# Attention's start in a fused Trainium2 kernel: fewer maxima ahead of the loop, mask rows in short packets

## The chip, the cores and the metric

One core of one Trainium2 chip. The metric is device time in microseconds (us), the median of three runs. A core has five engines with a queue each: PE (TensorE, matrix products), DVE (VectorE), ACT (ScalarE), POOL (GpSimd) and SP (SyncE, which here only issues DMAs). ACT and POOL issue DMAs too. Each works through its own instructions in the order in which they were written, and waits on semaphores for the others.

## The reference, cut to what matters

```
x = x + 0.5 * ffn(layernorm(x))     # x: (8, 256, 256), float32
x = x + attn(layernorm(x))
x = x + 0.5 * ffn(layernorm(x))

attn: 16 heads of 16, 4 groups of keys and values (4 heads share one), causal
  q, k, v = xn @ Wq + bq, xn @ Wk + bk, xn @ Wv + bv
  p = softmax(where(key > query, -inf, q k^T / 4));  out = p v
ffn: 8 experts, the best one for each row
  (silu(x @ gate[e]) * (x @ up[e])) @ down[e] * sigmoid(router score)
```

## The kernel before

The program has three stages: a first layer of experts, attention, a second layer of experts. Each expert layer (`ffn_pe`, `ffn_act`, `ffn_dve`, `ffn_pool`) gathers the rows of an expert in tiles of 128, multiplies them by weights that stay in SBUF, and scatters the result; it is PE's stage. The change leaves its products alone and touches its two borders with attention.

Attention goes through 8 batches b of 256 rows, with 4 groups of heads each, so 32 groups m, n = 0 to 31. For one batch, before any group of it:

- layernorm gives `xn`, `ln_transpose` (PE, L534) turns it, `ln_evacuate` (ACT, L542) copies it out of PSUM;
- `a_proj_q` (L1261) and `a_proj_kv` (L1269) are the projections, in float32; ACT adds the bias to the queries (`a_split_act`, L1296), DVE to the keys (`a_split_k`, L1327); the values' half goes by ACT (`a_vt_act`, L1279) and back to PE (`a_vt_pe`, L1286), and DVE adds their bias (`a_split_v`, L1332);
- queries and keys are split into three bfloat16 parts each (`a_split_act2`, L1307 and L1309; `a_split_dve2`; `a_split_act3`; `a_split_dve3`, L1348), and SP and ACT lay the parts one above the other with DMAs, "stacks" (`a_stack_q`, L1358, `a_stack_k`, L1366): 96 rows of `Qs` and `Ks`, in a ring of three batches.

For one group of heads, first the row maxima: `a_max_pe(m, k)` for k = 0, 1, 2 is one chunk of scores into one of two banks (two L1421 and an L1423 for the causal mask, or four L1414 and an L1418), `a_max_dve(m, k)` reduces it (L1451 or L1447). When a batch's maxima are there they are negated and turned (`a_neg_dve`, `a_neg_pe` L1468, `a_neg_copy` L1480), and SP puts them into row 103 of `Qs` (`a_max_row`, L1397). Rows 96 to 102 of `Qs` and 96 to 103 of `Ks` are constant "mask rows", `qrows` and `krows`, which SP loads once from HBM (L1624, L1625). Then the scores proper over all 104 rows, less maxima and mask: `a_scores(n, u)`, u = 0, 1, 2 (L1499), the exponentials (`a_exp`, ACT, L1506, the first with a table load), the causal cut on POOL (`a_mask`), the product with the values (`a_values`, L1527 and L1530), ACT's copy, PE's transposes (`a_heads_pe`, L1556), and DVE's division and addition into `xt` (`a_heads_sum`, `_div`, `_add`, L1576).

The order is written out by hand, for each engine apart. Ahead of the loop come the maxima of seven groups, m = 0 to 6, with the preparation of batches 1 and 2 between them. Then the loop: step n has the scores of group n + 1, the values of n, and the maxima of m = n + 7. A batch's stack must have landed before its first maxima (`a_max_pe` waits on `a_qs`).

SP's queue at attention's start: batch 0 of the first layer's result (`load_middle(0)`, L1611), as soon as the scatters of all but the last tile have landed; after the last scatter (`s_fin`) batches 1 to 4; stack 0; batches 5 to 7; the two mask rows; stack 1; then maxima rows and stack 2.

The scores of a group wait for the mask rows by one line:

```
                    if (m, k) == (NG + 1, 2):
                        pe.wait_ge(s_one, 32)
                        pe.wait_ge(a_v, 2)
                        for u in range(3):
                            a_scores(0, u)
```

Of the kernel before, what the change touches and what calls it, by code (L numbers as in the profile page):

```python
# [33 lines left out]
BA = 5  # L34
# [21 lines left out]
MAX_ORDER = (1, 0, 2)  # L56

EARLY = 3
WARM_MID = 5
WARM_NEXT = 26  # L60
WARM_FRONT = 7
# [78 lines left out]
def block_rows():  # L140
# [4 lines left out]
    return q, k  # L145


def macaron(nc, x, wq, bq, wkv, bk, bv, router, wall, constf, constb, qrows, krows,
            out):
    with ExitStack() as ctx:  # L150
# [147 lines left out]
        s_one = sem("s_one")  # L298
        dve = sem("dve")
# [497 lines left out]
        def warm(n, ps=bank[3]):  # L797

            for i in range(n):
                nc.tensor.matmul(ps[:], identb, cstb("mask"), start=True, stop=True)  # L800
# [171 lines left out]
        def ffn_gate_up(l, j, off):  # L972
# [6 lines left out]
            for m, done in ((0, f_gp), (1, f_up)):  # L979
# [12 lines left out]
                last.then_inc(done[l], 1)  # L992

# [67 lines left out]
        def ffn_pe(l):  # L1061
# [41 lines left out]
        def ffn_act(l):  # L1103
# [34 lines left out]
            for j in range(NP):  # L1138
                if j == 0:
# [3 lines left out]
                    else:  # L1143
                        ln_evacuate(2, B - 1, bank[4])
# [23 lines left out]
        def first_norm(seen):  # L1168


            for t in range(*tiles(1, 0)):
                ln_sums(1, t, seen)
# [4 lines left out]
        def ffn_dve(l, seen):  # L1177
# [40 lines left out]
            for j in range(NP):  # L1218
                if l == 1 and j == 0:
                    normalise(l, 0)  # L1220
# [81 lines left out]
        def a_split_act2(b):  # L1302
# [4 lines left out]
            a.copy(qp[:, b % 2, 0], q32[:]).then_inc(a_qh, 1)  # L1307
            a.wait_ge(a_k32, b + 1)
            a.copy(kp[:, b % 2, 0], k32[:]).then_inc(a_qh, 1)  # L1309

# [129 lines left out]
        def a_max_dve(m, k):  # L1440
# [8 lines left out]
            else:  # L1449
                h0 = HG * g + 2 * (u - 1)  # L1450
                v.tensor_reduce(mxa[:, b % 2, 1, h0:h0 + 2],  # L1451
                                o[:].rearrange("p (h k) -> p h k", h=2), AX.X, ALU.max).then_inc(a_am, 1)

# [131 lines left out]
        def _(sp):  # L1585
# [27 lines left out]

            load_middle(0)
            sp.wait_ge(s_fin[0], 1)
# [14 lines left out]
            a_stack_k(sp, 1, 2)  # L1630
            a_max_row(sp, 0)
# [10 lines left out]
        def _(p):  # L1642
# [10 lines left out]
            ln_apply(3, p)  # L1653
            a_split_dve2(2, p)
            a_split_dve3(2, p)
            a_mask(0)
            for n in range(NG * B):
                if n + 1 < NG * B:
                    a_mask(n + 1)
                b, g = divmod(n, NG)  # L1660
# [15 lines left out]
        def _(a):  # L1676
# [22 lines left out]
            a_split_act2(1)  # L1699
# [6 lines left out]
            a_vt_act(2, PRO_KV[2])  # L1706
            a_split_act2(2)
            a_split_act3(2)
# [311 lines left out]
```

## Time and profile before

| | |
|---|---|
| median of 3 runs | 404.71 us (404.37 to 405.14) |
| the profiled execution | 407.15 us |
| its span, first to last instruction | 405.4 us |
| mean granted TensorE clock | 0.977 of full |
| PE busy | 367.1 us (91%) |
| DVE busy | 241.9 us (60%) |
| ACT busy | 144.0 us (36%) |
| POOL busy | 172.7 us (43%) |

The profile is one execution; all its times count from the start of its span. A busy share is an average over stages: the first expert layer runs to about 126 us, attention from there to about 294 us, the second layer to the end. Matmuls are pipelined, so a row's duration is longer than the distance to the next row's start; the distance is what an instruction costs PE. A value in square brackets behind a row is how long the engine sat idle before it, and what ended that.

### The profile page before, as it was taken

The page shows a single profiled execution, that of the slowest core. Times are in us where ns is not written, and L with a number is a line of the kernel's source. Part 1 is how long each engine was busy: PE and PEld are TensorE (multiplying, and loading weights), DVE is VectorE, ACT ScalarE, POOL GpSimd, SP SyncE. Part 2 cuts the span into 40 slices and gives each one's busy share as a digit, 9 for nine tenths or more (in the row PEclk, how much of TensorE's full clock was granted, in tenths as well). Part 3 has the DMA queues.
Part 4 walks back from the last instruction along what each step waited for, and adds up shares of the span by engine and source line. Part 5 has one row for each costly group of instructions (what it writes and reads, how often), then busy time and mean ns, then how long its engine had stood idle before and what let it go on. Part 6 is the DMA issues. An engine that isn't in the chain of part 4 may idle for free.

```text
span 405.4 us, 8372 instructions
## 1 busy us (share of the span) xinstructions
PE 367.1 (91%) x3128; PEld 291.2 (72%) x3134; DVE 241.9 (60%) x725; ACT 144.0 (36%) x296; POOL 172.7 (43%) x284
## 2 busy tenths in 40 slices
PE   8999999999994868989999999998799999999980
PEld 6769999999962445646666565654499999999660
DVE  5889943222214656877878778889847875222220
ACT  3222111111111332776676657677334111111110
POOL 1040425544121252665867664565822214653111
PEclk9999999999999997999999999999989999999995
DMA  8969841279301761312314042200121102398100
GB/s 263 408 205 384 295 154 59 74 262 320 145 25 47 197 155 49 100 42 57 83 45 125 11 116 71 59 28 28 52 66 34 46 21 60 90 361 321 44 24 15
DMA packets 27055, 50.04 MB, mean 123 GB/s; under 512 B 4458, under 2 KB 20590, under 8 KB 25975
## 3 DMA queue, kind: packets, MB, share of 16 engines
q1 hardware_dynamic: 19118, 25.10, 19.4%
q0 software_dynamic: 4512, 21.50, 15.5%
q10 hardware_dynamic: 3376, 2.80, 2.3%
q8 instruction: 29, 0.48, 0.5%
q14 instruction: 20, 0.16, 0.1%
HBM read 35.16 MB, written 6.55 MB: 103 GB/s over the span
## 4 chain that ended last, share of the span: by engine, by line
PE 69%; DVE 16%; DMA 5%; issue 4%; SPq 2%; ACT 1%; POOL 1%; ACTq 1%; POOLq 0%; DVEq 0%
PE bank L990 26%; PE bank L1035 13%; PE bank L1527 3%; PE bank L1499 3%; PE bank L1261 3%; PE bank L1421 3%; DVE mxa L1451 2%; PE bank L534 2%; PE bank L1007 2%; PE bank L957 2%; PE bank L1414 2%; PE bank L1556 2%; PE bank L584 1%; DVE area L1576 1%; PE bank L1530 1%
## 5 line engine op out<-in xcount | busy, mean ns | idle before, releaser
L990 PEld LDWEIGHTS bank<-area,W 128*128 128x128 f32 x1024 | 120.6, 194 | 2.5 <-ACT area L1111 1.1
L990 PE MATMUL bank<-area,W 128*128 128x128 f32 x1024 | 121.5, 277 | 0.2 <-ACT area L1111 0.2
L1201 DVE TENSOR_TENSOR area<-area,bank 128x512 f32<-128x512 f32 x34 | 23.4, 688 | 68.2 <-issue 52.7
L1506 ACT ACTIVATE area<-bank 128x512 f32<-128x512 f32 x96 | 54.1, 597 | 23.1 <-PE bank L1499 22.6
L1035 PE MATMUL bank<-W,area 128*128 128x256 f32 x256 | 61.0, 381 | 0.4 <-DVE area L1186 0.4
L1515 POOL TENSOR_SCALAR_AFFINE_SELECT area<-area 128x512 f32<-128x512 f32 x64 | 40.9, 653 | 39.0 <-ACT area L1506 38.7
L1122 ACT ACTIVATE area<-bank 128x512 f32<-128x512 f32 x34 | 20.3, 597 | 101.8 <-PE bank L990 93.2
L1035 PEld LDWEIGHTS bank<-W,area 128*128 128x128 f32 x256 | 46.1, 190 | 6.8 <-issue 1.8
L1451 DVE TENSOR_REDUCE mxa<-bank 128x2 f32<-128x512 f32 x64 | 42.9, 672 | 9.3 <-PE bank L1423 9.1
L884 POOL DMA_INDIRECT x2d<-area,sidx x17 | 17.1, 1008 | 55.7 <-DVE area L1186 55.7
L884 POOL DMA_INDIRECT out<-area,sidx x17 | 17.1, 1007 | 52.9 <-DVE area L1186 52.1
L1186 DVE SCALAR_TENSOR_TENSOR area<-bank,ms,area 128x256 f32<-128x256 f32 x34 | 16.4, 481 | 30.8 <-PE bank L1035 26.2
L1499 PE MATMUL bank<-area 104*128 104x512 bf16 x96 | 34.7, 380 | 0.0
L1111 ACT COPY area<-bank 128x256 f32<-128x256 f32 x34 | 12.7, 372 | 55.0 <-PE bank L957 55.0
L872 POOL DMA_INDIRECT area<-x,gidx x18 | 18.5, 1029 | 29.9 <-DVE sidx L691 20.0
L1447 DVE TENSOR_REDUCE mxa<-bank 128x4 f32<-128x512 f32 x32 | 22.0, 688 | 12.7 <-PE bank L1434 12.0
L1421 PE MATMUL bank<-area 96*128 96x256 bf16 x128 | 25.7, 284 | 0.7 <-DVE mxa L1451 0.3
L872 POOL DMA_INDIRECT area<-rows,gidx x18 | 17.5, 974 | 14.2 <-PE bank L990 7.6
L1527 PE MATMUL bank<-area,V 128*32 128x256 f32 x256 | 20.5, 390 | 0.6 <-issue 0.6
L534 PE MATMUL bank<-cf,area 128*128 128x128 f32 x96 | 15.4, 284 | 4.8 <-DVE area L519 2.6
L542 ACT COPY area<-bank 128x512 f32<-128x512 f32 x16 | 9.4, 586 | 26.4 <-PE bank L534 26.3
L1421 PEld LDWEIGHTS bank<-area 96*128 96x128 bf16 x128 | 9.0, 100 | 13.4 <-DVE mxa L1447 5.1
(198 smaller groups left out, 568.3 us busy)
## 6 DMA issues: line engine op xcount, KB each, us to landing
W<-wall SPq DMA_DIRECT2D x24, 512.0 KB, 6.9
area<-area SPq DMA_DIRECT2D x48, 128.0 KB, 2.4
area<-x SPq DMA_DIRECT2D x8, 256.0 KB, 5.3
area<-x2d SPq DMA_DIRECT2D x8, 256.0 KB, 3.0
rows<-area ACTq DMA_DIRECT2D x8, 256.0 KB, 2.4
area<-JV SPq DMA_DIRECT2D x40, 32.0 KB, 1.9
cb<-constb ACTq DMA_DIRECT2D x1, 296.0 KB, 4.4
area<-x,gidx POOLq DMA_INDIRECT x18, 3.4
```

Source lines behind the costliest of these rows:

```text
L534: last = nc.tensor.transpose(o[:, c, i * P:(i + 1) * P], src[:, i, c * P:(c + 1) * P], ident)
L872: nc.gpsimd.indirect_dma_start(dst, None, table, bass.IndirectOffsetOnAxis(ap=gidx[:, bass.ds(j, 1)], axis=0)).then_inc(done, 16)
L884: nc.gpsimd.indirect_dma_start(ffn_out[l], bass.IndirectOffsetOnAxis(ap=sidx[:, bass.ds(t, 1)], axis=0), ob[:, j % OB, :], None, bounds_ch ...
L990: last = pe.matmul(ps[:, i * P:(i + 1) * P], W[:, w:w + P], xT[:, j % 2, c, :], start=(c == 0), stop=(c == C - 1))
L1035: last = pe.matmul(ps[:, 0:H], hT[:, n % 2, i, :], W[:, bass.ds(off + at, H)] if mixed(l, n) else W[:, off + at:off + at + H], start=(i == ...
L1201: v.tensor_tensor(out, sil[:, n % 2, :], bank[2 + n % 2][:], ALU.mult).then_inc(f_h[l], 1)
L1421: pe.matmul(o[:, h * S:(h + 1) * S], Qs[0:KROWS, r, HG * g + 2 * (u - 1) + h, P:S], Ks[0:KROWS, r, g, :], start=(h == 0), stop=False)
L1451: v.tensor_reduce(mxa[:, b % 2, 1, h0:h0 + 2], o[:].rearrange("p (h k) -> p h k", h=2), AX.X, ALU.max).then_inc(a_am, 1)
L1499: pe.matmul(o, Ks[0:MROWS + 1, r, g, k0:k0 + P], rhs, start=True, stop=True).then_inc(a_st, 1)
L1506: a.activation(PT[:, n % 2, u * 512:(u + 1) * 512], bank[u][:], ACT.Exp, scale=D ** -0.5).then_inc(a_e, 1)
L1515: p.affine_select(out=src, in_=src, compare_op=ALU.is_ge, fill=0.0, base=0, pattern=[[0, HG], [1, P]], channel_multiplier=-1).then_inc(a_p ...
L1527: pe.matmul(bank[5][32 * h:32 * h + 32, c0:c0 + S], V[:, b % VB, 0, g, :], PT[:, n % 2, h * S:(h + 1) * S], start=True, stop=False, tile_p ...
```

## The change

It has seven parts, all at attention's borders:

1. PE and DVE do the maxima of four groups (m = 0 to 3) ahead of the scores of group 0, not seven. The three first steps are written out (`early_step_pe`, `early_step_dve`), with two groups of maxima each; from n = 3 on the loop is the old one.
2. The scores of group 0 wait for three mask-row DMAs (`s_one` of 48). They are cut into packets of 2 KB (`ROWX`); `krows` and the first batch's `qrows` are issued behind `load_middle(0)`, the rows of the other two batches behind stack 1 and the loads of batches 5 to 7, which are themselves behind stack 1 now.
3. PE does the first two chunks of maxima ahead of batch 1's transposes.
4. ACT adds the bias of batches 1 and 2's keys (`a_split_k_act`), not DVE.
5. ACT does the exponentials of group 0 ahead of splitting batch 2; POOL its first mask ahead of that batch's `a_split_dve2`.
6. At the end of the first layer DVE's `ln_sums` of batch 0 come ahead of the last `finish`.
7. At the start of the second layer DVE's `normalise(1, 0)` comes ahead of the last group's heads, PE's last `ln_transpose` between the gate and the up products of tile 0, and ACT's last `write_rows` behind `copy_tile(0)`.

```diff
@@ block_rows
-    return q, k
+    return (x.reshape(len(x), -1, ROWX).transpose(1, 0, 2) for x in (q, k))
@@ ffn_gate_up
                 last.then_inc(done[l], 1)
+                if l == 1 and j == 0 and m == 0:
+                    ln_transpose(2, B - 1, bank[4])
@@ ffn_pe
                         warm(2, bank[2])
-                    else:
-                        ln_transpose(2, B - 1, bank[4])
@@ ffn_act
                     else:
+                        write_rows(a, B - 1)
                         ln_evacuate(2, B - 1, bank[4])
@@ ffn_dve
+            if l == 0:
+                for t in range(*tiles(1, 0)):
+                    ln_sums(1, t, seen)
             finish(NP - 1)
@@ new, scalar
+        def a_split_k_act(b, ps):
+            a = nc.scalar
+            a.wait_ge(a_kv, b + 1)
+            a.wait_ge(a_qr, 2 * b)
+            a.activation(k32[:], ps[0:NG * D, 0:S], ACT.Identity, bias=bk_s[:]).then_inc(a_k32, 1)
@@ new, tensor
+        def early_step_pe(n):
+            pe = nc.tensor
+            groups = early_groups(n)
+            a_scores(n + 1, 0)
+            if n == 0:
+                pe.wait_ge(a_ms, 2)
+                ln_transpose(1, 3, PRO_T[3])
+            a_max_pe(*groups[0])
+            if n == 0:
+                a_vt_pe(2, PRO_KV[2])
+            if n == 2:
+                pe.wait_ge(a_v, 4)
+                a_neg_pe(2)
+            a_scores(n + 1, 1)
+            if n == 1:
+                a_vt_pe(3)
+            a_max_pe(*groups[1])
+            a_scores(n + 1, 2)
+            a_max_pe(*groups[2])
...
@@ sync
+            def load_qrows(r0, r1):
+                n = NH * S // ROWX
+                sp.dma_start(Qs[KROWS:MROWS, r0:r1].rearrange("o r h s -> o (r h s)").rearrange(
+                    "o (c x) -> o c x", x=ROWX), qrows[n * r0:n * r1].rearrange("c o x -> o c x")).then_inc(s_one, 16)
             load_middle(0)
+            sp.wait_ge(s_used, 1)
+            sp.dma_start(Ks[KROWS:MROWS + 1].rearrange("o r g s -> o (r g s)").rearrange("o (c x) -> o c x", x=ROWX),
+                         krows.rearrange("c o x -> o c x")).then_inc(s_one, 16)
+            load_qrows(0, 1)
             sp.wait_ge(s_fin[0], 1)
...
-            for b in range(BA, B):
-                load_middle(b)
-            sp.dma_start(Ks[KROWS:MROWS + 1].rearrange("o r g s -> o (r g s)"), krows).then_inc(s_one, 16)
-            sp.dma_start(Qs[KROWS:MROWS].rearrange("o r h s -> o (r h s)"), qrows).then_inc(s_one, 16)
             a_stack_q(sp, 1, 0)
             a_stack_k(sp, 1, 0, slice(2, 3))
             a_stack_q(sp, 1, 1)
             a_stack_q(sp, 1, 2)
             a_stack_k(sp, 1, 2)
+            for b in range(BA, B):
+                load_middle(b)
+            load_qrows(1, QB)
             a_max_row(sp, 0)
@@ scalar
             a_split_act(2, PRO_Q[2])
-            a_vt_act(2, PRO_KV[2])
-            a_split_act2(2)
-            a_split_act3(2)
-            ln_evacuate(1, 3, PRO_T[3])
             for u in range(3):
                 a_exp(0, u)
+            a_split_act2(2, PRO_KV[2])
+            a_vt_act(2, PRO_KV[2])
@@ tensor
             warm(WARM_NEXT)
-            ln_transpose(1, 1, PRO_T[1])
             a_vt_pe(0, PRO_KV[0])
             for m in range(NG):
                 for k in range(3):
                     a_max_pe(m, k)
                     if (m, k) == (0, 1):
+                        ln_transpose(1, 1, PRO_T[1])
                         a_proj_q(1, PRO_Q[1])
...
+            pe.wait_ge(s_one, 48)
+            pe.wait_ge(a_v, 2)
+            for u in range(3):
+                a_scores(0, u)
+            a_neg_pe(1)
+            for n in range(RAMP):
+                early_step_pe(n)
+            for n in range(RAMP, NG * B):
```

How the order changes, at three places. Line numbers in the changed kernel differ (L1266 and L1274 are the projections, L1291 `a_vt_pe`, L537 the layernorm's transposes, L1427 to L1436 the maxima, L1581 the scores, L1550 `a_neg_pe`). First PE's queue behind the fill products of attention's start, before:

```order
L800 MATMUL bank<-cb 128x512 x26
L534 MATMUL bank<-cf,area 128x128 x4
L1286 MATMUL bank<-cf,vT 128x64 x2
L1421 MATMUL bank<-area 128x256 x2
L1423 MATMUL bank<-cb 128x2x128
L1414 MATMUL bank<-area 128x128 x4
L1418 MATMUL bank<-cb 128x512
L1261 MATMUL bank<-area,wq_s 128x256 x4
```

and in the changed kernel:

```order
L803 MATMUL bank<-cb 128x512 x26
L1291 MATMUL bank<-cf,vT 128x64 x2
L1434 MATMUL bank<-area 128x256 x2
L1436 MATMUL bank<-cb 128x2x128
L1427 MATMUL bank<-area 128x128 x4
L1431 MATMUL bank<-cb 128x512
L537 MATMUL bank<-cf,area 128x128 x4
L1266 MATMUL bank<-area,wq_s 128x256 x4
```

The four transposes of batch 1 went from ahead of the first two chunks of maxima to behind them, right ahead of the projection that reads them.

Second, SP's queue, from the first loads to the first row of maxima, before:

```order
L1611 DMA area<-x2d 128x2x256 x5
L1358 DMA area<-area 16x8x512 x3
L1366 DMA area<-JV 16x4x256 x2
L1358 DMA area<-area 16x8x512 x3
L1611 DMA area<-x2d 128x2x256 x3
L1624 DMA area<-krows 8x3072
L1625 DMA area<-qrows 7x12288
L1358 DMA area<-area 16x8x512 x3
L1366 DMA area<-JV 16x4x256
L1358 DMA area<-area 16x8x512 x3
L1366 DMA area<-JV 16x4x256
L1397 DMA area<-mT 1x8x256
```

and in the changed kernel:

```order
L1693 DMA area<-x2d 128x2x256
L1703 DMA area<-krows 8x3x1024
L1698 DMA area<-qrows 7x4x1024
L1693 DMA area<-x2d 128x2x256 x4
L1371 DMA area<-area 16x8x512 x3
L1379 DMA area<-JV 16x4x256 x2
L1371 DMA area<-area 16x8x512 x6
L1379 DMA area<-JV 16x4x256
L1371 DMA area<-area 16x8x512 x3
L1379 DMA area<-JV 16x4x256
L1693 DMA area<-x2d 128x2x256 x3
L1698 DMA area<-qrows 7x8x1024
```

One third of the query mask rows went ahead of stack 0; three loads and the other two thirds went behind stack 1. The row of maxima (L1410 there) comes next.

Third, ACT's queue from batch 2's queries on, before:

```order
L1296 ACTIVATE area<-bank,bq_s 128x256 x2
L1279 COPY vT<-bank 64x256
L1307 CAST area<-area 128x512
L1309 CAST JV<-k 64x256
L1314 CAST area<-area 128x512
L1316 CAST JV<-kr 64x256
L542 COPY area<-bank 128x512
L1506 ACT_TABLE_LOAD
L1506 ACTIVATE area<-bank 128x512 x6
```

and in the changed kernel:

```order
L1301 ACTIVATE area<-bank,bq_s 128x256 x2
L1588 ACT_TABLE_LOAD
L1588 ACTIVATE area<-bank 128x512 x3
L1312 CAST area<-area 128x512
L1322 ACTIVATE k<-bank,bk_s 64x256
L1316 CAST JV<-k 64x256
L1284 COPY vT<-bank 64x256
L1588 ACTIVATE area<-bank 128x512
L545 COPY area<-bank 128x512
```

Batch 2's values (the COPY to `vT`) and its first split stand behind three exponentials now, with the keys' bias (L1322) between them.

## Rows read from the trace of the kernel before

**Rows 1.** Stretches: start:end, length, busy us of each engine, PEclk (granted clock), DMA share, GB/s

```profile
142.00:147.00 5.00, 4.94 (x36) 4.04 (x35) 3.53 (x14) 2.04 (x4) 1.61 (x9) 1.00 0.78 204
147.00:151.00 4.00, 0.45 (x4) 0.20 (x2) 2.11 (x4) 1.02 (x3) 3.56 (x6) 1.00 0.51 84
152.00:158.00 6.00, 5.52 (x23) 3.44 (x21) 3.90 (x9) 0.59 (x1) 1.84 (x2) 0.50 0.31 83
161.50:181.50 20.00, 17.92 (x165) 10.71 (x165) 15.81 (x37) 14.46 (x30) 12.82 (x16) 1.00 0.24 63
199.00:216.70 17.70, 16.69 (x175) 11.12 (x174) 14.39 (x41) 11.87 (x27) 12.42 (x25) 1.00 0.29 82
```

**Rows 2.** Timeline of PE, 141 to 186 us: start, duration, instruction

```profile
141.74 0.66 PE L534 MATMUL bank<-cf,area 128*128 128x128 f32 x4 [1.58 <-DVE area L519]
142.59 0.39 PE L1421 MATMUL bank<-area 96*128 96x256 bf16 x2
...
143.38 1.89 PE L1261 MATMUL bank<-area,wq_s 128*128 128x256 f32 x8
...
150.78 0.34 PE L1286 MATMUL bank<-cf,vT 64*128 64x64 f32 x2 [3.55 <-ACT vT L1279]
...
160.85 0.27 PE L1423 MATMUL bank<-cb 128*128 128x256 bf16 x1
...
165.30 0.81 PE L1499 MATMUL bank<-area 104*128 104x512 bf16 x3
...
185.86 0.42 PE L1527 MATMUL bank<-area,V 128*32 128x256 f32 x4
```

**Rows 3.** Timeline of ACT at attention's start; ACTq is its DMA issues

```profile
142.43 0.59 ACT L542 COPY area<-bank 128x512 f32<-128x512 f32 x1 [2.90 <-PE bank L534]
...
147.01 0.40 ACT L1309 CAST JV<-k 64x256 bf16<-64x256 f32 x1 [0.22 <-DVE k L1327]
147.44 2.82 ACTq L1366 DMA_DIRECT2D area<-JV  x2
...
151.71 1.20 ACTq L1366 DMA_DIRECT2D area<-JV  x2
...
166.44 3.33 ACT L1506 ACTIVATE area<-bank 128x512 f32<-128x512 f32 x6
```

**Rows 4.** Timeline of SP's DMA issues

```profile
122.81 0.38 SPq L1611 DMA_DIRECT2D area<-x2d  x1
...
140.77 1.67 SPq L1611 DMA_DIRECT2D area<-x2d  x3
142.94 0.29 SPq L1625 DMA_DIRECT2D area<-qrows  x1
```

**Rows 5.** DMA packets of 142.5:144 (first two) and 144:146 us (last two)

```profile
DMA packets 517, 0.50 MB, mean 333 GB/s; under 512 B 29, under 2 KB 517, under 8 KB 517
q1 hardware_dynamic: 517, 0.50, 100.6%
...
DMA packets 276, 0.46 MB, mean 230 GB/s; under 512 B 27, under 2 KB 261, under 8 KB 269
q1 hardware_dynamic: 276, 0.46, 111.3%
```

**Rows 6.** DMA issues of 122 to 125.5 us: KB each, median us from issue to landing

```profile
area<-x2d SPq DMA_DIRECT2D x1, 256.0 KB, 2.7
```

**Rows 7.** Timeline of DVE: last tile, first row of maxima, two reductions

```profile
125.93 0.48 DVE L1186 SCALAR_TENSOR_TENSOR area<-bank,ms,area 128x256 f32<-128x256 f32 x1 [3.39 <-PE bank L1031]
126.33 0.74 DVE L381 BATCH_NORM_STATS2 bn<-area 128x6 f32<-128x256 f32 x2
...
153.25 0.27 DVE L1480 COPY mT<-bank 8x256 bf16<-8x256 bf16 x1
...
167.76 1.29 DVE L1451 TENSOR_REDUCE mxa<-bank 128x2 f32<-128x512 f32 x2
```

**Rows 8.** Timeline of DVE at the second layer's start

```profile
293.14 0.41 DVE L1165 TENSOR_SCALAR area<-area,ms 128x256 f32<-128x256 f32 x1
```

More of the change, by code:

```diff
@@ L56 @@
 MAX_ORDER = (1, 0, 2)
+ROWX = 1024
 EARLY = 3
@@ L60 @@
 WARM_NEXT = 26
+RAMP = 3
 WARM_FRONT = 7
@@ L799, in warm @@
             for i in range(n):
-                nc.tensor.matmul(ps[:], identb, cstb("mask"), start=True, stop=True)
+                last = nc.tensor.matmul(ps[:], identb, cstb("mask"), start=True, stop=True)
+            return last
         def idle(n):
@@ L1168, in first_norm @@
         def first_norm(seen):
-            for t in range(*tiles(1, 0)):
-                ln_sums(1, t, seen)
             ln_stats(1, 0, seen)
@@ L1452, in a_max_dve, with early_groups, early_step_dve @@
                                 o[:].rearrange("p (h k) -> p h k", h=2), AX.X, ALU.max).then_inc(a_am, 1)
+        def early_groups(n):
+            return [(NG + 2 * n + i, k) for i in range(2) for k in range(3)]
+        def early_step_dve(n, seen):
+            for i, (m, k) in enumerate(early_groups(n)):
+                a_max_dve(m, k)
+                if (n, i) == (0, 0):
+                    a_split_v(2, PRO_KV[2])
+                if (n, i) == (1, 0):
+                    a_split_k(3)
+                if (n, i) == (1, 1):
+                    a_split_v(3)
+                if (n, i) == (2, 0):
+                    a_neg_copy(2)
+                    a_heads_sum(0, seen)
+                if (n, i) == (2, 1):
+                    a_heads_div(0, seen)
+                if (n, i) == (2, 2):
+                    a_heads_add(0, seen)
+            if n == 1:
+                a_neg_dve(2)
+                a_split_dve2(3)
+            if n == 2:
+                round_stats_next(0, seen)
+                round_aggr(0, seen)
+                round_eps(0, seen)
+                round_guess(0, seen)
+        def early_step_pe(n):
[8 more added lines that the diff above has]
+                a_vt_pe(2, PRO_KV[2])
+            if n == 2:
+                pe.wait_ge(a_v, 4)
+                a_neg_pe(2)
+            a_scores(n + 1, 1)
+            if n == 1:
+                a_vt_pe(3)
+            a_max_pe(*groups[1])
+            a_scores(n + 1, 2)
+            a_max_pe(*groups[2])
+            if n == 0:
+                pe.wait_ge(a_q32, 3)
+                a_proj_q(3, bank[7], (0,))
+                a_max_pe(*groups[3])
+                pe.wait_ge(a_v, 3)
+                a_values(0)
+                a_proj_q(3, bank[7], (1,))
+                a_max_pe(*groups[4])
+                a_proj_kv(3)
+            else:
+                a_values(n)
+                a_max_pe(*groups[3])
+                a_max_pe(*groups[4])
+            a_max_pe(*groups[5])
+            if n >= 1:
+                pe.wait_ge(a_q32, 4)
+                a_heads_pe(n - 1)
         def a_neg_dve(e):
@@ L1737, in _ @@
                     ln_evacuate(1, b + 4, bank[6])
-            write_rows(a, B - 1)
             ffn_act(1)
@@ L1797, in _ @@
             a_neg_dve(1)
-            a_split_k(2, PRO_KV[2])
-            for m in range(NG, NG + 3):
-                for k in range(3):
-                    a_max_dve(m, k)
-                    if (m, k) == (NG, 0):
-                        a_neg_copy(1)
-                    if (m, k) == (NG, 2):
-                        a_split_v(2, PRO_KV[2])
-            for n in range(NG * B):
+            a_neg_copy(1)
+            for n in range(RAMP):
+                early_step_dve(n, seen)
+            for n in range(RAMP, NG * B):
                 b, g = divmod(n, NG)
@@ L1857, in _ @@
                 a_heads_add(n, seen)
+                if n == NG * B - 2:
+                    normalise(1, 0)
             ffn_dve(1, seen)
@@ L1995 @@
     cf, cbf = constants()
+    qrows, krows = block_rows()
     import ml_dtypes
```

41 lines of the change are left out of this document (16 added, 25 removed).

## The prediction, made before the changed kernel ran

> **What bounds the kernel now.** I read the stretches first, then each engine's timeline where a stretch is thin. In the loop PE is busy 16.69 of 17.70 us for one batch at full clock and DVE 14.39 [rows 1]: PE's work sets that pace, and the loop from n = 3 on isn't changed, so what the change gains or loses must arise ahead of step 3 or at the two borders, and the loop hands it on in full. The thin stretch is 147 to 151 us, with 0.45 us of PE work; from 152 to 158 the granted clock is 0.50, so PE runs at 1.2 GHz, the lower of its two levels, behind that gap [rows 1]. PE's timeline shows the gap as one wait of 3.55 us for ACT's copy of the values [rows 2]. ACT had issued two DMAs ahead of it, which took 2.82 us; a later pair took 1.20 [rows 3]. The query mask rows went out at 142.94, shortly before [rows 4].
>
> How heavy those rows are follows from the packets. In 142.5 to 144, 517 packets fill 16 engines: 24 engine-us, 0.047 each. In 144 to 146, 276 packets fill 111.3% of 32, 35.6 engine-us; 269 of them at 0.047 make 12.6, so the 7 of over 8 KB take 23, about 3.3 us each [rows 5]. They run until about 148.5, and the stacks of batch 1 (issued from 146.8) meet them. I take the 1.6 us (2.82 less 1.20) for their doing.
>
> **The change, part by part,** as shifts against the old times.
>
> *DVE's sums ahead of the last `finish`.* `load_middle(0)` goes out at 122.81 and takes 2.7 [rows 4, 6]: the data is there at 125.5. Two sums take 0.74; `finish` starts at 126.25, not 125.93 [rows 7]. The last scatter, and the loads and stack 0 behind it, come **0.3 later**.
>
> *Chunks ahead of batch 1's transposes.* The first chunks can't start before stack 0, so at 142.6 + 0.3 = 142.9. Two chunks take 0.79 (142.59 to 143.38), so the transposes start at 143.7. ACT's copy now starts 0.7 behind the transposes' start (141.74, 142.43) and takes 0.59 [rows 2, 3]: the projection starts at 143.7 + 1.35 = 145.05, **1.7 later**. Before, that copy lay beside the chunks.
>
> *Keys by ACT.* ACT's cast of the keys (147.01) was waiting 0.22 for DVE [rows 3]. Its own 0.48 in line adds **0.3**. So the cast is at 149.0, and with 0.43 to the issue and 1.20 for the pair without the stall the values' copy starts at 150.6, PE's `a_vt_pe` at 151.05, against 150.78. The stall's 1.6 are eaten by the 2.0: **0.3 later**.
>
> *The clock.* PE's gap there is now about 2 us (a projection that starts 1.7 later ends later too), so I take full clock for what follows. From 150.78 to the last chunk of m = 3 (160.85, over at 161.1) are 10.3 us [rows 2]. The 5.52 us of busy time at 0.50 would be half, 2.8 [rows 1]; a little of that comes back as waits for DVE. I take **2.6 earlier**. PE is through with m = 3 at 161.1 + 0.3 - 2.6 = 158.8.
>
> *The mask rows behind stack 1.* The scores of group 0 now follow at once and wait for all three mask DMAs. The last is issued so: the first row of maxima at 153.25 [rows 7] as before (0.3 later, 0.25 earlier by the clock), 1.1 for DVE's V and third part of the queries, 1.2 for two stack issues, then 1.67 for three loads [rows 4]: 157.2. Its landing isn't in the trace. Below, it isn't faster than a load, 2.7 [rows 6]; above, the old one, about 5.6 (142.94 to 148.5). It carries two thirds of the bytes to the same 7 partitions, 2/3 of 3.3 = 2.2, behind loads that end some 2.1 behind its issue: 4.3. I take that, nearer the old row, since it is the same transfer cut smaller: it lands at 161.5, and PE **waits 2.7**. The first row of maxima is issued behind it and does not come sooner.
>
> The Trainium skill (DMA: Bandwidth & Descriptors, "Why a DMA increments its semaphore by 16 and not by 1") says that a DMA is spread by the outermost dimension of its two sides, and that is 7 partitions here, in 2 KB packets too; then the landing is the 4.3. Were the packets spread over all 16 engines, the landing would be a load's 2.7 and the sum 1.6 lower.
>
> *The ramp.* Before, from the first scores (165.30) to the values of group 4 (185.86) are 20.56 us [rows 2], with 17 chunks of maxima between them (the rest of m = 6, m = 7 to 10, two of m = 11). Now there are 23 (m = 4 to 10, two of 11). Six more cost 6 x 0.395 = 2.4; the transposes of batch 3, `a_vt_pe(2)` and `a_neg_pe(1)`, which stood ahead of the scores, bring 0.44, 0.27 and 0.22 of PE work: 3.3. To this come waits that the old order didn't have. `a_vt_pe(2)`, in the first early step, waits for ACT, which has three exponentials (3.33 / 6 = 0.55 each), a cast of the queries (an estimate: the same 128x512, 0.55), the keys (0.48) and the 0.4 cast ahead of the copy [rows 3]: with 0.4 for the scores, 3.5 us after their start, when PE has had 1.9 of work: 1.6. `a_vt_pe(3)` waits for DVE's keys behind a chunk, about 1. And an early step holds six reductions of 0.65 (two in 1.29) [rows 7] and three small operations, some 4.3 us of DVE, beside some 3.9 of PE: 0.4 in each of two steps. Sum: 20.56 + 3.3 + 2.6 + 0.8 = 27.3, so the values of group 4 start at 161.5 + 27.3 = 188.8, against 185.86: **2.9 later**. Bounds of the ramp: 21.8 (without waits: PE idles 2.1 of 20 us in the old stretch [rows 1], so 20.56 + 3.3 - 2.1) to 29.
>
> *The second layer's start.* `normalise(1, 0)` at 293.14 [rows 8] stood behind the last heads, 0.6 of DVE; ahead of them it brings the first product up to 0.6 forward. But the last transposes, 0.44, then lie between products instead of beside ACT's copy. **0.1 earlier**; bounds 0 and 0.6. `write_rows` moves on ACT behind a copy and is wanted two tiles later, nothing.
>
> *The clock again.* PE now sits idle 2.7 us for the mask rows and has waits on both sides. A gap of 3.55 brought the lower level [rows 1, 2]; a gap of this size may. It would cost between 0 and the 2.6 above; I take **0.6**, little, since ACT and DVE pace part of that stretch.
>
> Sum: 2.9 - 0.1 + 0.6 = **+3.4 us**. Against the profiled execution's 407.15 that is 410.55; it lies 2.44 above the median of 404.71, so for the median 408.1.
>
> **The rivals.**
>
> *A. The ramp runs at PE's pace (faster).* If the mask rows have landed by 158.8 and the extra chunks fill the waits for exponentials, the ramp is its lower bound and half of the old waits, 22.8: the values of group 4 start at 181.6, 4.3 earlier, and with the border's 0.1 that is 400.3. For it speaks that the old stretch mostly lacks ready work, not PE time. Against it: ACT's queue puts batch 2 behind group 0. It decides where the last mask rows land within 1.6 us of their issue, sooner than any load here. Chance 0.12.
>
> *B. The mask rows come in time, the ramp's waits remain.* A landing of 2.7 or less leaves 1.1 of the wait: +1.8; with no clock loss, +1.2: 405.9. Chance 0.2.
>
> *C. The stall isn't the packets' doing (the change doesn't do what it says), or it comes back behind the new mask rows.* The pair on ACT takes 2.82 again, PE's gap is 3.6, and the clock falls once more: 1.6 and up to 2.6 on top, less what the wait for the mask rows hides (2.7, all but 1.5): +4.9: 409.6, and up to 411. Against: the seven long packets are gone. Chance 0.18.
>
> The forecast keeps 0.5.
>
> **How the numbers follow.** The predicted time is the forecast's, 408.1. Its own range, from the landing (2.7 to 5.6) and the clock (0 to 2.6), is 405.9 to 411. B and C lie almost inside; A doesn't. The range of 8 in 10 is 405.0 to 411.0. A measurement of this kernel tells 0.2%, 0.8 us, from no change. Faster by that: A, 0.12. Within it: the low end of B, 0.08. Slower: 0.80.
>
> **What would show it.** Right: PE's wait for the mask rows ahead of the first scores, 2 to 3 us, at 158 to 159; the pair of DMAs on ACT near 1.2; batch 1's first projection near 145; `a_vt_pe(2)` waiting for ACT; the values of group 4 near 188.8; after that the same 17.7 us a batch. Wrong: scores of group 0 that start before 159.5 without a wait, or values of group 4 before 186. If the first is seen and the time is still longer, the ramp's waits alone were the price (B).

## The result, and the profile after

The changed kernel takes 414.54 us (median of 4 runs, 411.98 to 417.0), against 404.92 for the kernel before (404.37 to 406.98, 4 runs): ratio 1.020, 95% interval 1.015 to 1.025, **9.6 us slower**. (The ratio is the comparison's own estimate, with its interval; the quotient of the two medians is 1.024, inside the interval.) The forecast was 3.4 slower, 408.1, with 405.0 to 411.0: right in sign, outside the range.

The profiled execution of the changed kernel took 413.78 us (span 411.9), 0.8 below its median; that of before, 407.15 (span 405.4), lay 2.2 above its own median. So the two traces differ by 6.5 us only; the other 3.0 of the 9.6 are the distances of the two profiled executions from their medians, and no trace shows what makes them.

Stretches of the changed kernel, with the columns of [rows 1]:

```profile
126.00:132.00 6.00, 3.75 (x22) 1.45 (x12) 3.77 (x18) 0.53 (x1) 0.98 (x1) 0.75 0.08 22
...
147.00:151.00 4.00, 1.80 (x15) 1.23 (x13) 2.91 (x5) 2.49 (x7) 3.43 (x7) 1.00 0.29 78
...
152.70:156.50 3.80, 3.65 (x17) 2.65 (x18) 3.17 (x7) 0.58 (x1) 0.98 (x1) 0.55 0.49 131
...
160.00:163.40 3.40, 0.00 (x0) 0.01 (x1) 0.77 (x2) 0.41 (x1) 0.00 (x0) 0.96 0.13 21
163.40:174.00 10.60, 10.53 (x49) 5.55 (x50) 3.24 (x6) 6.41 (x14) 7.18 (x9) 0.53 0.28 75
...
212.60:230.30 17.70, 16.70 (x177) 11.12 (x174) 14.36 (x40) 11.86 (x27) 12.40 (x25) 1.00 0.29 80
```

The loop is what it was: 16.70 us of PE in 17.70. New is that PE stands still for 3.4 us at 160 and then does nearly all of the next 10.6 us of the ramp at 1.2 GHz (their mean granted clock is 0.53). From 152.7 to 156.5 the mean is 0.55. PE's timeline of the same kernel:

```profile
142.73 0.39 PE L1434 MATMUL bank<-area 96*128 96x256 bf16 x2 [1.76 <-DMA area<-area]
...
144.79 1.99 PE L1266 MATMUL bank<-area,wq_s 128*128 128x256 f32 x8 [0.68 <-ACT area L545]
...
150.96 0.34 PE L1291 MATMUL bank<-cf,vT 64*128 64x64 f32 x2 [2.20 <-ACT vT L1284]
...
159.59 0.27 PE L1436 MATMUL bank<-cb 128*128 128x256 bf16 x1
163.42 1.44 PE L1581 MATMUL bank<-area 104*128 104x512 bf16 x3 [3.55 <-DMA area<-mT]
...
194.10 0.64 PE L1609 MATMUL bank<-area,V 128*32 128x256 f32 x8
```

Against [rows 2]: the projection of batch 1 starts at 144.79 (143.38), `a_vt_pe(1)` at 150.96 (150.78), the first scores at 163.42 (165.30), the values of group 4 at 194.10 (185.86). ACT's pair of DMAs takes 1.29 us instead of the 2.82 of [rows 3]:

```profile
149.15 1.29 ACTq L1379 DMA_DIRECT2D area<-JV  x2
```

SP's queue has the loads, the last mask rows and the row of maxima in this order, behind stack 1:

```profile
155.50 1.62 SPq L1693 DMA_DIRECT2D area<-x2d  x3
157.16 0.37 SPq L1698 DMA_DIRECT2D area<-qrows  x1
157.58 0.76 SPq L1410 DMA_DIRECT2D area<-mT  x1
```

**The ledger of the two traces**, in changes of length from landmark to landmark (PE's timeline): first layer up to the last down product +0.6 (123.93 to 124.56, where nothing is changed); from there to the first chunk of maxima -0.5; to `a_vt_pe(1)` 0.0; to the first scores -2.1 (12.46 for 14.52); **to the values of group 4 +10.1** (30.68 for 20.56); the loop -0.3; from the last values to the second layer's first down product -1.4; the rest 0.0. Sum +6.5. The -1.4 is the clock, not the order: in before the first 32 gate and up products ran at 1.2 GHz for most of their length, here none did. First before, then the changed kernel:

```profile
294.00:298.00 4.00, 3.98 (x22) 3.74 (x20) 3.59 (x20) 2.24 (x3) 0.60 (x1) 0.57 0.47 135
```

```profile
302.00:306.00 4.00, 4.00 (x35) 4.00 (x36) 3.59 (x20) 1.45 (x2) 1.52 (x2) 1.00 0.43 133
```

### The profile page after: what moved, and what is told of

Its sections match the earlier page's. It is cut to its first block, busy times and chain, and to the rows that moved or that the text cites. A ratio compares the mean times of both kernels' runs of the same rounds, so it can differ in the third digit from the quotient of the medians.

```text
span 411.9 us, 8362 instructions
## 1 busy us (share of the span) xinstructions
PE 371.8 (90%) x3125; PEld 292.5 (71%) x3125; DVE 240.7 (58%) x723; ACT 144.2 (35%) x298; POOL 171.6 (42%) x284
## 4 chain that ended last, share of the span: by engine, by line
PE 65%; DVE 15%; DMA 7%; issue 4%; ACT 4%; SPq 2%; POOL 1%; ACTq 0%; POOLq 0%; DVEq 0%
PE bank L994 25%; PE bank L1041 13%; DVE mxa L1464 3%; PE bank L1581 3%; PE bank L1266 3%; PE bank L1434 3%; PE bank L1609 3%; PE bank L961 2%; PE bank L537 2%; DMA x2d<-area,sidx 2%; PE bank L1638 1%; DMA area<-mT 1%; PE bank L1427 1%; DMA area<-x2d 1%; PE bank L575 1%
## 5 line engine op out<-in xcount | busy, mean ns | idle before, releaser
L994 PEld LDWEIGHTS bank<-area,W 128*128 128x128 f32 x1024 | 119.0, 192 | 3.0 <-ACT area L1115 1.5
L994 PE MATMUL bank<-area,W 128*128 128x128 f32 x1024 | 120.1, 275 | 0.7 <-ACT area L1115 0.6
L1581 PE MATMUL bank<-area 104*128 104x512 bf16 x96 | 36.1, 395 | 3.5 <-DMA area<-mT 3.5
L537 PE MATMUL bank<-cf,area 128*128 128x128 f32 x96 | 16.7, 302 | 1.9 <-DVE mT L1562 1.6
```

Of the source, the lines that this page charges most:

```text
L537: last = nc.tensor.transpose(o[:, c, i * P:(i + 1) * P], src[:, i, c * P:(c + 1) * P], ident)
L994: last = pe.matmul(ps[:, i * P:(i + 1) * P], W[:, w:w + P], xT[:, j % 2, c, :], start=(c == 0), stop=(c == C - 1))
L1581: pe.matmul(o, Ks[0:MROWS + 1, r, g, k0:k0 + P], rhs, start=True, stop=True).then_inc(a_st, 1)
```

## The experiments

All times come as ratios to the kernel before on the same chip in the same set, since its median moved between sets (406.3 to 410.8 us). The ratios are the comparison's estimates; the quotient of two medians differs from them by up to 0.4% (before_fill: 402.68 by 406.49, 0.991), so a difference of that size between two kernels is no more than a hint. "Ramp" is from the first scores to the values of group 4, "head" from the first chunk of maxima to those values, both from the kernel's profiled execution. Last column: where its trace shows the granted clock at half, 140 to 180 us. A "fill product" (`warm`) is a matrix product of 128x512 whose result nobody reads; it only keeps PE busy, 0.22 us each at full clock. "Theory A" to "E" are those of the expectations.

| kernel | ratio (95%) | ramp | head | half clock from (us) |
|---|---|---|---|---|
| before | 1 | 20.56 | 43.27 | 151.2 |
| changed | 1.020 (1.015 to 1.025) | 30.68 | 51.37 | 152.9, 163.1 |
| rows_first | 1.017 (1.013 to 1.020) | 31.05 | 49.86 | 147.0, 157.2, 167.4 |
| fill_scores | 1.029 (1.024 to 1.034) | 27.68 | 49.79 | 147.2, 157.4 |
| rows_fill | 1.019 (1.015 to 1.023) | 27.69 | 48.43 | 143.8, 157.4 |
| before_rows | 1.009 (1.005 to 1.012) | 20.70 | 43.17 | 152.4, 162.6 |
| new_ramp | 1.013 (1.003 to 1.023) | 27.47 | 45.38 | 152.7 |
| old_ramp | 1.003 (0.998 to 1.007) | 20.57 | 46.45 | 144.7, 155.0, 165.2 |
| borders | 1.002 (0.998 to 1.006) | 20.48 | 42.30 | 144.1, 154.4 |
| before_fill | **0.994** (0.990 to 0.998) | 20.49 | 39.49 | none |
| after_fill | 1.008 (1.004 to 1.013) | 27.67 | 47.66 | 143.2 |
| rows_fill_before | 1.003 (1.000 to 1.007) | 20.55 | 43.33 | 164.5 |
| new_ramp_fill | 1.002 (0.998 to 1.005) | 27.48 | 41.81 | none |
| more_fill | 0.993 (0.990 to 0.997) | 20.49 | 39.49 | none |
| max_row_first | 1.000 (0.996 to 1.004) | 20.49 | 42.96 | 154.1 |
| max_row_fill | **0.993** (0.989 to 0.996) | 20.50 | 39.49 | none |
| no_part3 | 1.004 (1.000 to 1.008) | 27.84 | 43.73 | 152.8 |
| no_part3_fill | 1.000 (0.997 to 1.004) | 27.68 | 43.51 | none |
| next_fill | 1.013 (1.009 to 1.017) | 27.97 | 46.36 | 151.7 |
| row_fill_next | 0.995 (0.992 to 0.998) | 20.49 | 39.49 | none |

A profiled execution is one of the runs, and not always a typical one: that of rows_first lies 4.0 us above its kernel's median, of old_ramp 3.0, of before 2.2 (against 404.92), of after_fill 1.9, and that of row_fill_next 2.7 below; the others lie within 1.4.

### The wait ahead of the first scores

rows_first, on the changed kernel:

```diff
-            for b in range(BA, B):
-                load_middle(b)
             load_qrows(1, QB)
             a_max_row(sp, 0)
+            for b in range(BA, B):
+                load_middle(b)
```

> The changed kernel with the last mask rows and the first row of maxima issued ahead of the loads of batches 5 to 7 (same DMAs, other order on SP). The changed kernel ran at 414.5, with a wait of 3.55 us ahead of the first scores and 10.2 us at a granted clock of 0.5 right behind it. Theory A (the wait for the rows opens the gap, and the gap costs the clock): the wait all but goes (rows issued at about 155.5 instead of 157.2, nothing ahead of them), 3.5 us, and with it most of the low clock, 3 to 4: 407 to 408. Theory B (only the wait, the clock falls anyway): 411. Theory C (the early steps are paced by ACT's and DVE's queues, so that a sooner start is given back in them): 413 or more, first scores at 160 but the values of group 4 no sooner than 192.

fill_scores, and rows_fill (the edit above and `warm(4, ...)`):

```diff
+            warm(16, bank[0])
             pe.wait_ge(s_one, 48)
             pe.wait_ge(a_v, 2)
             for u in range(3):
```

> The changed kernel with 16 fill products (128x512, 0.22 us each at full clock, 3.5 us) on a free bank ahead of the wait for the mask rows; nothing else is moved. PE is then busy where it was idle for 3.55 us. Theory A (the idle gap lowers the clock for the ramp): first scores still at 163.4, but the ramp runs at full clock: 414.5 less 3 to 4.5, 410 to 411.5. Theories B and C (the low clock isn't that gap's doing, or isn't what paces the ramp): 414 to 415.

> Both: rows first and 4 fill products (0.9 us) ahead of the first scores. Theory A: what is left of the wait is filled: 407 to 408, and less spread between runs than the 412 to 417 of the changed kernel. Theory B: 411 to 412. Theory C: 413 to 414.

Measured 1.017, 1.029, 1.019: none came near theory A's 407 to 411. The wait is gone in all three, and in fill_scores and rows_fill the ramp ran at full clock in 27.7 us, 3.0 less than the changed kernel's: that gap did bring the low clock of the ramp. The times are nearest to theory C's (413 or more), but its mechanism, a ramp held by ACT's and DVE's queues, is not what the traces show. All three have the low clock earlier instead, at 144 to 147 and at 157. fill_scores, although its ramp is as short, is the slowest kernel of all. The fill isn't too long for the wait: from `a_vt_pe(1)` to the first scores it takes 12.29 us, 12.46 in the changed kernel. What is longer is the way from the first chunk to `a_vt_pe(1)`, 9.82 against 8.23, with half clock from 147.2; and in its trace the first chunk was already 2.6 later, behind projections at half clock. That is one execution; whether the timed runs lost their time in the same places is not shown. The wait ahead of the scores was only a part of the cost.

### One part at a time, on the kernel before

before_rows is part 2 alone; new_ramp parts 1 and 5 alone; old_ramp all but these two; borders parts 6 and 7. Their edits are pieces of the change's diff. before_fill is new:

```diff
                     if (m, k) == (1, 1):
+                        warm(9, bank[0])
                         a_vt_pe(1, PRO_KV[1])
```

> The kernel before with part 2 of the change alone: mask rows in packets of 2 KB, the first third and krows early, loads of batches 5 to 7 and the rest behind stack 1. Its first scores come later than in the changed kernel (165.3), so the rows are in time. If the long packets made the stall: ACT's pair of DMAs takes 1.2 instead of 2.82, PE's gap shrinks from 3.55 to about 2, 1.6 us sooner, and up to 2.6 more from the clock: 401 to 403.5 against 404.9. If the stall is something else: the pair takes 2.8 again and the time is 404.5 to 405.5.

> The kernel before with parts 1 and 5 of the change alone: four groups of maxima ahead, three written-out steps, ACT's exponentials and POOL's mask of group 0 ahead of splitting batch 2. Mask rows, transposes, keys and both borders as before. At full clock the new ramp took 27.7 us from the first scores to the values of group 4 in two kernels, against 20.56 before, and the first scores come about 4.5 sooner (9 chunks of 0.395 and 0.9 of other work). Theory D (the ramp is the price): ratio to before 1.007 to 1.013 (2.6 for the order, and up to 2.6 for a clock that falls more often in it). Theory E (the new ramp is harmless, the rest of the change does it): 0.998 to 1.002.

> The changed kernel without parts 1 and 5: the old ramp, and parts 2, 3, 4, 6 and 7 of the change. Part 2 alone measured a ratio of 1.009 to before. Theory D: what is left beside the ramp is part 2's and part 3's: 1.008 to 1.013. Theory E: 1.02, as the changed kernel.

> The kernel before with parts 6 and 7 alone (sums ahead of the last finish; second layer's start). By the prediction +0.3 and -0.1, ratio 1.000 (0.999 to 1.001). If the second layer's start is worth more than I took (from the last values to the first down product the changed kernel needed 12.99 us against 14.42 before, of which the lower clock there is 1.7): no more than 0.998. If the sums ahead of the last finish bring the lower clock at 129 us (it was there in all five profiles of kernels with after's start, and not in that of before): 1.003 to 1.006.

> The kernel before with 9 fill products (0.22 us each, 1.9) on a free bank in PE's gap ahead of a_vt_pe(1) (3.55 us), nothing else. If that gap is what lowers the clock behind it in before too: no stretch at 0.50 between 151 and 158, and a ratio of 0.994 to 0.998. If the lower clock comes from the whole of the thin stretch or elsewhere as well: 0.998 to 1.002, and stretches at 0.50 at other places.

The ramp alone costs 1.3%, with a wide interval (four runs): theory D. The borders cost nothing that can be told (1.002, interval over 1); the low clock at 129 isn't part 6's doing, since before_fill, without part 6, has it too, from 129.3. Part 2 alone costs 0.9%, though ACT's stall is gone (pair 1.22 us, `a_vt_pe(1)` 6.59 us behind the first chunk instead of 8.19): neither expectation had that.

old_ramp missed both theories, and the miss matters. It holds parts 2, 3, 4, 6 and 7, and its trace has part 2's stall (DVE waits 1.46 us for the row of maxima, see below) and part 3's half clock at 144.7. Theory D had 1.008 to 1.013; it measured 1.003, and its interval ends at 1.007. So the prices of parts below, taken with the new ramp or alone, don't add up in the old one. Why not stays open.

One group of fill products makes the kernel before faster: at 148 to 151 PE is now busy, and what follows runs at 2.4 GHz, where [rows 1] has a granted clock of 0.50:

```profile
148.00:151.00 3.00, 3.00 (x20) 1.47 (x19) 2.49 (x5) 1.42 (x4) 2.40 (x7) 1.00 0.43 93
151.00:158.00 7.00, 5.85 (x40) 4.25 (x40) 5.40 (x11) 1.89 (x5) 4.11 (x4) 1.00 0.40 108
```

### The same parts with the clock held

The fill ahead of `a_vt_pe(1)` added to the changed kernel (with rows first), to part 2, and to the ramp; and two more fills for before (`WARM_NEXT` 31, and `warm(6, bank[0])` ahead of the second layer).

> The changed kernel with the last mask rows and the row of maxima ahead of the loads of batches 5 to 7, and 8 fill products ahead of a_vt_pe(1), where it waits 2.2 us. The fill alone took before from 406.5 to 402.7 (ratio 0.994). If what the changed kernel pays beyond the ramp's order is the clock: ratio 0.998 to 1.005 (0.994 plus the ramp's 2.1 to 2.9 us). If it pays something else as well: 1.010 or more.

> Part 2 alone on the kernel before, with the same 8 fill products. Part 2 alone measured 1.009, although its stall on ACT was gone and PE reached a_vt_pe(1) 1.6 sooner. If that was paid by the clock alone, the fill takes it back: 0.990 to 0.995. If part 2 itself costs: 0.998 or more.

> Parts 1 and 5 alone on the kernel before, with 9 fill products ahead of a_vt_pe(1): the new order of the ramp with the clock held there. Against the same fill in the old order (0.994), the order's own price is 2.1 to 2.9 us if my sum of it was right: 0.999 to 1.001. If the ramp costs by its lower clock only: 0.994 to 0.996. From first scores to the values of group 4: 27.3 to 27.7 us at full clock.

> The kernel before with 9 fill products ahead of a_vt_pe(1), 31 instead of 26 ahead of batch 1's transposes (PE waits 1.2 to 1.6 us there) and 6 ahead of the second layer (PE waits 1.6). If every thin stretch draws the lower clock: below the 0.994 of the one fill, 0.988 to 0.993, none at 0.50 around 294. If the further fills only delay what stands behind them: 0.995 to 0.998.

**The ramp's order.** With the clock at 1.00 in both, new_ramp_fill's head is 41.81 us against before_fill's 39.49: its ramp is 27.48 against 20.49, and its first scores come 4.67 sooner. That is 2.3 us; the timed ratios, 1.002 against 0.994, say 0.8%, 3.3 us, with intervals of 0.34% and 0.39% to either side. PE's timeline of new_ramp_fill shows where a ramp at full clock waits: for ACT's values of batch 2 (0.74), DVE's keys of batch 3 (1.09), and DVE's reductions ahead of group 4 (1.39):

```profile
157.13 0.81 PE L1577 MATMUL bank<-area 104*128 104x512 bf16 x3
...
160.66 0.33 PE L1287 MATMUL bank<-cf,vT 64*128 64x64 f32 x2 [0.74 <-ACT vT L1280]
...
168.84 0.31 PE L1287 MATMUL bank<-cf,vT 64*128 64x64 f32 x2 [1.09 <-DVE k L1336]
...
182.01 0.39 PE L1430 MATMUL bank<-area 96*128 96x256 bf16 x2 [1.39 <-DVE mxa L1460]
...
184.61 0.64 PE L1605 MATMUL bank<-area,V 128*32 128x256 f32 x8
```

**Part 2.** With the fill it still costs 0.9% (1.003 against 0.994). The trace of rows_fill_before says how, in DVE's timeline and in PE's:

```profile
163.93 0.28 DVE L1483 COPY mT<-bank 16x256 bf16<-16x256 bf16 x1 [2.48 <-DMA area<-mT]
```

```profile
164.86 0.61 PE L1424 MATMUL bank<-area 96*128 96x256 bf16 x2 [2.81 <-DVE mxa L1450]
165.26 0.42 PE L1426 MATMUL bank<-cb 128*128 128x256 bf16 x1
165.47 1.06 PE L536 MATMUL bank<-cf,area 128*128 128x128 f32 x4
```

The first row of maxima was issued at 158.28, behind three loads and the mask rows (before_fill: 155.15). DVE's next copy into the same `mT` waits for it, DVE's reductions queue behind that copy, PE's chunks behind those, and the clock is at half when PE goes on (0.61 for a pair that takes 0.39 at full clock).

**more_fill** is no better than one fill, and the six products ahead of the second layer do harm there: last values to first down product 14.09 us, 12.81 in before_fill.

### The row of maxima, and part 3

max_row_first and max_row_fill are before_rows and rows_fill_before with this edit:

```diff
+            a_max_row(sp, 0)
+            load_qrows(1, QB)
             for b in range(BA, B):
                 load_middle(b)
-            load_qrows(1, QB)
-            a_max_row(sp, 0)
```

> Part 2 alone as in before_rows (1.009), but with the first row of maxima issued directly behind stack 1, ahead of the last mask rows and of the loads of batches 5 to 7. In the profile of part 2 with fill, DVE's copy of the next row of maxima waited 2.48 us for that DMA and PE's maxima waited 2.81 for DVE. If that is part 2's cost: the waits go, and the ratio is 0.997 to 1.002. If part 2 costs by something else (the early mask rows, packets of 2 KB): 1.006 to 1.010 again.

> The same with 8 fill products ahead of a_vt_pe(1). If the row of maxima was part 2's cost: 0.990 to 0.995, no worse than the fill alone (0.994), against 1.003 with the row behind the loads. Otherwise 1.000 to 1.004.

1.000 and 0.993, against 1.009 and 1.003: the place of the row of maxima in SP's queue was part 2's cost, as far as these ratios tell. (The edit takes the last mask rows ahead of the loads as well, but in none of the four traces does PE wait ahead of the first scores, so it isn't they that were late.) In max_row_fill the row is issued at 155.09, DVE's copy does not wait, and the head is the 39.49 of before_fill:

```profile
155.09 0.76 SPq L1400 DMA_DIRECT2D area<-mT  x1
155.89 0.46 SPq L1619 DMA_DIRECT2D area<-qrows  x1
156.39 1.39 SPq L1614 DMA_DIRECT2D area<-x2d  x3
```

max_row_first shows something else. Its mask rows go in packets of 2 KB, and still ACT's pair of DMAs stalls, as it did in before, and PE waits for it:

```profile
150.74 2.48 ACTq L1369 DMA_DIRECT2D area<-JV  x2
...
153.73 0.34 PE L1289 MATMUL bank<-cf,vT 64*128 64x64 f32 x2 [3.21 <-ACT vT L1282]
```

Neither mask rows nor loads were in flight ahead of it: between 146 and 150.7 the trace has a single DMA packet.

no_part3 is rows_first with batch 1's transposes back ahead of the first chunks, no_part3_fill has the 8 fill products too, next_fill is rows_first with `WARM_NEXT` 34, row_fill_next is max_row_fill with `WARM_NEXT` 31.

> The changed kernel with rows first (1.0167), and with part 3 undone: batch 1's transposes are again ahead of the first chunks. By its order part 3 costs 1.7 us; if it also brings the lower clock at 143 to 150, 1 to 2 more: 1.008 to 1.012, no stretch at 0.50 between 140 and 150. If only the 1.7: 1.012 to 1.013. If part 3 costs nothing: 1.016 to 1.018.

> The changed kernel with rows first, part 3 undone and 8 fill products ahead of a_vt_pe(1): the ramp's new order is then all that is left beside the fill. The same ramp on the kernel before measured 1.002 with the fill: 1.000 to 1.004 if parts 4, 6 and 7 are worth nothing either way; against 1.008 with part 3. At 1.007 or more part 3 isn't to blame.

> The changed kernel with rows first (1.0167) and 34 instead of 26 fill products ahead of the first chunks, where PE waits 1.6 to 2.2 us for stack 0 (8 x 0.22 = 1.7). If part 3's cost beyond its order's 1.7 us is the clock that this wait brings down: 1.006 to 1.011 and no stretch at 0.50 between 140 and 150. If the clock falls there for other reasons, or the rest of part 3's cost is no clock: 1.015 to 1.018.

> The kernel before with part 2, the first row of maxima ahead of the loads, 8 fill products ahead of a_vt_pe(1) (0.993), and 31 instead of 26 ahead of batch 1's transposes. If every thin stretch counts: 0.988 to 0.992. If the first fill had all that there is: 0.992 to 0.995.

**Part 3** costs 1.3% with the new ramp (rows_first 1.017, no_part3 1.004), with the fill 0.8% (1.008, 1.000): 3.3 to 5 us. That is more than expected: for no_part3 the lowest expectation was 1.008. after_fill's 1.008 lies between its two theories. In the old ramp it can't be so much (old_ramp, above). The stretch 143.2 to 150 of after_fill and of no_part3_fill, which differ by part 3 alone:

```profile
143.20:150.00 6.80, 5.71 (x20) 4.28 (x21) 2.04 (x10) 0.58 (x1) 2.78 (x13) 0.50 0.01 2
```

```profile
143.20:150.00 6.80, 6.37 (x39) 4.42 (x39) 5.25 (x16) 2.71 (x7) 3.26 (x13) 1.00 0.13 34
```

At half clock PE got through 20 instructions instead of 39. Ahead of it PE had waited 2.27 us for stack 0, and waited another 0.67 for ACT's copy in it; in no_part3_fill the four transposes sit in that wait. Of the seven kernels with part 3 five show half clock that begins between 143 and 147; the two that don't are the changed kernel's profiled execution and next_fill, which fills the wait. Of the thirteen without part 3 one does. next_fill bears this out in part: its clock is at 1.00 from 143 to 150, and it is 0.4% faster than rows_first; but 0.9% slower than no_part3, where the order explains 0.4% (the 1.7 us of the forecast), and its 1.013 lies between the two expectations. What the other 0.5% is, beyond the width of two intervals, stays open; its trace has a longer stretch at half clock behind `a_vt_pe(1)`.

**Which gap brings the clock down.** In all twelve kernels without fill products ahead of `a_vt_pe(1)` PE waits there 1.9 to 3.6 us, and a stretch at half clock begins between 151 and 158. In the eight with them it waits at most 0.5 us, and none has such a stretch. The length of a gap doesn't settle it alone: ahead of attention's first fill products, at 128 to 130 us, PE waits 2.0 to 2.8 us in all twenty traces; seventeen have half clock from about there, three have not, the kernel before (a wait of 2.45) among them.

## Why the prediction was wrong, step by step

The step that failed is the clock: the forecast had PE gain 2.6 us from it ahead of the scores and lose 0.6 in the ramp; in the traces PE gained 1.4 and lost 3.2. The order of the work came nearly as forecast.

- *DVE's sums, +0.3.* `finish` starts at 126.61, and the last down product was 0.63 late by itself: 0.05. Smaller, no matter.
- *Chunks ahead of the transposes, +1.7.* Transposes at 143.52 (143.7), projection at 144.79 (145.05): in this trace the step is right. What it left out is the idle time that the order makes: moving the transposes behind the chunks left waits of 1.76 and 0.68 us beside them, and in most traces with part 3 the clock falls there. With the new ramp part 3 measured 3.3 to 5 us.
- *Keys by ACT, the stall gone.* Pair 1.29 (1.20), `a_vt_pe(1)` at 150.96 (151.05). Right in size, but **the mechanism is not borne out**: I took the 1.6 us of stall for the long packets' doing. In six kernels that have them the pair took 2.82, 2.54, and four times 1.21 or 1.22; in fourteen with 2 KB packets thirteen times 1.2 to 1.3, and 2.48 in max_row_first. In before the last long packet was over at about 148.6, and the second DMA of the pair was stuck from 148.03 to 150.26. So long packets are neither needed nor enough, and part 2 can't be said to cure the stall. Its cause is open. In the three traces with a stall a fetch of instructions (16 KB, queue q8) starts within 0.1 us of the pair's second issue; in five without one it starts 0.34 to 0.36 us behind it. No run tests that.
- *The clock, -2.6.* **Failed: 1.4.** I took full clock behind a gap of about 2 us. The gap was 2.20, and the granted clock was at half again from 152.9, though for 3.4 us instead of 6.8. From `a_vt_pe(1)` to the end of m = 3 PE took 8.9 us (forecast 7.75, before 10.3) and was through at 159.9, not 158.8. The profile of before also had more to give back than its timed runs: holding the clock there is worth 3.8 us between the traces of before and before_fill (head), and 0.6% in the timed runs.
- *The mask rows, a wait of 2.7.* Issued at 157.16 (157.2). The scores started at 163.42 (161.5), a wait of 3.55, and the profile names the row of maxima (by the weights' load, the mask rows; which landed last the trace doesn't settle). The bytes came nearly when I had put them: the last DMA packet in that stretch ends at 161.8. PE went on 1.6 us later, and the term had nothing for that. I had written that the row of maxima "does not come sooner", and priced its lateness at nothing: alone, on the kernel before, it is part 2's 0.9%. In the changed kernel rows_first, which takes it forward, is only 0.3% faster, no difference that can be told. The Trainium skill (DMA: Bandwidth & Descriptors, "Two DMAs through the same engine are not ordered") says that the descriptors of one queue on one engine start in order; that agrees with the row of maxima, 4 KB, on which DVE waited in rows_fill_before until 5.7 us after its issue, behind 768 KB of loads.
- *The ramp, 27.3 us.* **Right**: 27.5 to 28.0 in the eight traces with its clock at or near 1.00, with the waits for ACT and DVE that the step named, though smaller for ACT (0.74, not 1.6) and larger ahead of group 4. Net of the earlier first scores it is 2.3 us.
- *Second layer, -0.1.* 12.99 us from the last values to the first down product, against 12.81 in before_fill at full clock: +0.2. Right that it is nothing.
- *The clock again, +0.6.* **Mis-sized**: the ramp took 30.68 where 27.5 is its length at full clock, 3.2; that is outside the step's own bounds of 0 to 2.6.

The sum in the terms of the two traces, which lie 6.5 apart: 3.4 forecast; 1.1 more because PE was through with m = 3 later; 0.9 for the longer wait; 2.8 for the ramp, of which the clock is 2.6; 0.3 less in the loop and 1.3 less at the second layer, where before's trace had the low clock and this one had not. That is 6.6. The other 3.0 of the 9.6 us lie between the traces and the medians, and no step accounts for them.

The timed runs give a ladder of their own: changed 1.020, rows first 1.017, with the fill ahead of `a_vt_pe(1)` 1.008, without part 3 1.000, and with the old ramp (max_row_fill, which also lacks parts 4, 6 and 7) 0.993. Its steps hold in this order only, as old_ramp shows.

Of the rivals, A fell (a ramp at full clock is 27.5, not 22.8), B fell with the wait. C was right in both halves, but not together: the stall isn't the packets' doing (max_row_first), and the clock falls once more, but in the changed kernel without the stall.

The Trainium skill (TensorE: Matmul & The Clock Gate, Part 1) says that the gate follows how busy PE has been recently. The traces agree, twelve of twelve kernels against none of eight; I used it for a gap of 3.55 us and took about 2 for short enough.

**A version that beats both.** before_fill, more_fill, max_row_fill and row_fill_next all lie 0.5 to 0.7% under the kernel before, 2 to 3 us, and their intervals exclude 1. They don't differ from each other. before_fill is one line. Six pairs of kernels differ by this fill alone, and in each the ratio is lower with it, by 0.4 to 1.1%.

## What to carry to other kernels

Where PE's granted clock stands at half behind a gap, try a few fill products in the gap before moving work, and price an edit that takes work out of a wait at that work and the clock. Don't take a stall out of one profile for a fixed cost: look whether other executions have it. Before a DMA goes to the end of a queue, look for who reuses its source as well as who reads its target: here the buffer `mT` held up DVE, and DVE held up PE. When a step takes a gain out of a profiled execution, check that the median run has it to give.

## What was not expected of the hardware

- The clock's stretches wander between runs of one kernel: four runs of the changed kernel had mean granted clocks of 0.976, 0.971, 0.964 and 0.956 and took 411.98, 413.78, 415.3 and 417.0 us, in that order. One profile is one draw; lengths at full clock (the head, 39.49 us in four kernels with the old ramp, to 0.01) are what can be compared.
- Making one gap shorter can leave the time as it was, when the clock falls at another thin place: before_rows reached `a_vt_pe(1)` 1.6 us sooner behind the first chunk and had its half clock at 152.4 and again at 162.6, and its head is 43.17 us, 43.27 before.
- The same DMA pair on ACT took 1.2 to 1.3 us in seventeen traces and 2.5 to 2.8 in three, with long packets and without.
- A DMA's size says little of its landing: a later row of maxima, 8 KB, took 1.8 us from issue to landing in the changed kernel, where the queue was free (issued at 184.95), while waiters of the first row, 4 KB, went on 5.8 us (the changed kernel's scores) and 5.7 us (DVE in rows_fill_before) after an issue behind three loads.
